# Four graph layers on one core: node tables beside the sort and in groups, with the near rows scattered behind all key rows

## The chip, the cores and the metric

One core of a Trainium2 chip runs the whole program. The metric is the device time of one execution in microseconds; the median over several executions is given.

## What is computed

Four graph layers run over N = 6250 nodes of 128 features and E = 206250 edges (src, dst, sorted by dst). The one whose start is changed is layer 0, whose softmax is over the edges of one source:

```python
x_i = x[dst]; x_j = x[src]
key = (x_i @ Wk + bk).reshape(-1, H, DH)
msg = (x_j @ Wm + bm).reshape(-1, H, DH)
query = (x_j @ Wq + bq).reshape(-1, H, DH) / jnp.sqrt(jnp.float32(DH))
scores = jnp.sum(query * key, axis=2)
smax = jax.ops.segment_max(scores, src, num_segments=N)
e = jnp.exp(scores - smax[src])
ssum = jax.ops.segment_sum(e, src, num_segments=N)
alpha = e / ssum[src] * cnt[src][:, None]
out = jax.ops.segment_sum((msg * alpha[:, :, None]).reshape(-1, D), dst, num_segments=N)
```

Layers 1 to 3 are an attention, a GAT and a weighted sum over the same edges, all summed by dst.

## The kernel before

Edges lie in SBUF as 128 partitions of T = 1612, once ordered by source (o = 0) and once by destination (o = 1). A pass (`pass_pool`, `pass_dve`, `pass_act`, `pass_sp`) walks along all partitions at once, in 62 turns of two halves of K = 13 edges. The row of the far end of each edge (k, q and m, and so on) is gathered by POOL, one indirect DMA per edge column, so 1612 in a pass (L1256). The row of the near end is the same along a segment: it stands once in a DRAM array of mostly zeros (`start_rows_by_src`, `start_rows_by_dst`), at the place of the segment's first edge, is read in order by SP (`near_load`) and is spread along the segment by a scan on DVE (`hold_rows`, L1312). Pass B runs by source and makes maximum and sum of each source; PA (same layer), P1, P2 and P3 run by destination.

Before pass B stands a preparation:

- `loads_sp`, `keys_dve`, `sort_dve`: keys (src, dst) are sorted by a bitonic network on 128 x 2048. DVE does the minima and maxima. For the steps across partitions PE turns the keys and ACT copies the half that DVE can't read from PSUM (`sort_act`, `sort_pe`, L709 and L723). There are 7 such stages (lp), each with two exchanges. The input is already sorted by dst, so a second sort (`unsorted`) is skipped.
- Beside it ACT, PE and SP make the q, k and m tables of layer 0 in 13 groups of 4 x 128 nodes (`proj0_sort_act`, `proj0_sp`). The order on ACT and PE is written out: `BEFORE_GROUP = {9: 1, 11: 2}` puts the exchanges of stage 1 ahead of group 9 and those of stage 2 ahead of group 11; the rest come behind group 12. SP writes zeros into the start-row array in between: 104 rows of 256 KB ahead of the groups (`zeros_sp`, L403), 5 behind each group, the rest behind the last.
- Behind the sort, `order_sp`, `order_dve`, `node_parts_dve`, `masks_dve` and `node_ends_dve` make the tables for each order: the restart masks of the scans, and for each of 6271 nodes where its segment begins (`spos`) and ends (`endix`). For this a node's partition is found by comparing the first key of each partition with all nodes (`cmp_n`, L1027 and L1029); that partition's key row (1612 int16) is gathered from DRAM by POOL, one gather for each 128 nodes (L1072), and ACT counts with a sign activation and accumulator how many keys lie below the node (`count_act`, L1077). By source the 52 gathers run in pairs of two buffers, with a staging copy of the index on POOL. By destination there is one gather and one count in each turn of pass B (L1262).
- `spread_sp` and `spread_pool` load q rows (before pass B) and k rows (behind it) back from DRAM and POOL scatters them, 49 x 128, to the beginnings of the segments (L1115).

Line 8 of `nodes_pool`, the wait that ties a pair of gathers to the counts two steps back, and in `pass_pool` the extra gather of pass B:

```python
g_.wait_ge(S(f"nt_counted{b}"), g * 2 + 2)
...
if q is PB and b:
    g_.wait_ge(S("nt_counted"), i + NB)
    g_.sem_inc(S("pool_go"), 1)
    g_.indirect_dma_start(row1, None, keyrow_t[1], bass.IndirectOffsetOnAxis(ap=row_i[:, 0:1], axis=0))
```

## Time and profile before

| | us |
|---|---|
| median of 3 executions | 11731.74 (11731.05 to 11731.93) |
| the profiled execution | 11731.4, its span 11729.7 |
| POOL busy, 8674 instructions | 8195.7 (70%) |
| DVE busy | 7246.8 (62%) |
| ACT busy | 5377.5 (46%) |
| PE busy | 1023.3 (9%) |
| first gather of pass B | at 772.29 |
| last key-row gather of pass B | at 2861.35 |
| first gather of pass A | at 3027.4 |

Time runs from the start of the span. "Busy" leaves out the time between two instructions of an engine, and for POOL each gather has 0.3 us of that. A timeline row has start, duration, engine, line, operation, and in brackets the idle time ahead of it and what ended it. The last part of the chain of waits (34% of the span) is POOL on L1256.

### The profile page before, as it was taken

The numbers are of one execution on the slowest core, as the hardware profiler recorded it, in microseconds if no ns is written. First come the engines' busy times: TensorE is split into PE (matmuls) and PEld (weight loads), VectorE is DVE, ScalarE is ACT, GpSimd is POOL, SyncE is SP. The second block draws the span as 40 slices with busy tenths as digits, with TensorE's granted clock in tenths as the row PEclk, the third lists the DMA queues.
The fourth block names the chain that finished last, engine by engine and source line by source line (L and its number), as shares of the span: only waits on it lengthen the run. The fifth ranks groups of instructions, "written<-read, shape, count | busy, mean of one in ns | idle before, by whom it ended". The sixth has DMA issues, their size and how long they took to land.

```text
span 11729.7 us, 40039 instructions
## 1 busy us (share of the span) xinstructions
PE 1023.3 (9%) x4194; PEld 843.3 (7%) x4194; DVE 7246.8 (62%) x7044; ACT 5377.5 (46%) x6052; POOL 8195.7 (70%) x8674
## 2 busy tenths in 40 slices
PE   4102222222000000040000000200000000000001
PEld 3002222222000000020000000200000000000001
DVE  9625555554588888848999999444444443333333
ACT  3134444443466666636666666233333333333332
POOL 0067777776777777747777776677777767777776
PEclk8555555555555555565555555555555555555555
DMA  7646666665466666636666666233333333333333
GB/s 260 221 148 209 204 211 207 206 211 173 145 213 213 214 214 214 213 103 211 223 221 222 222 222 208 71 112 113 112 111 112 112 95 105 105 105 105 105 105 105
DMA packets 791402, 1959.33 MB, mean 167 GB/s; under 512 B 213947, under 2 KB 419603, under 8 KB 790738
## 3 DMA queue, kind: packets, MB, share of 16 engines
q1 hardware_dynamic: 458010, 1136.08, 27.1%
q0 software_dynamic: 333184, 821.25, 25.2%
q14 instruction: 173, 1.42, 0.0%
q8 instruction: 35, 0.57, 0.0%
HBM read 1217.94 MB, written 738.73 MB: 167 GB/s over the span
## 4 chain that ended last, share of the span: by engine, by line
POOL 35%; DVE 19%; issue 15%; DMA 4%; PE 1%; ACT 1%; DVEq 0%; POOLq 0%; SPq 0%; ACTq 0%
POOL region L1256 34%; DVE work L1411 4%; DVE psB L1312 4%; DMA region<-x,ix_s 2%; DVE psR L1348 2%; DVE work L1344 2%; DVE psR L1404 2%; DVE psR L1396 2%; POOL work L1685 1%; PE psB L808 1%; DVE m_ext L1379 0%; POOL start_rows_by_dst L1115 0%; DVE psR L1357 0%; DMA region<-h,ix_s 0%; DVE psR L1382 0%
## 5 line engine op out<-in xcount | busy, mean ns | idle before, releaser
L1411 DVE TENSOR_TENSOR_SCAN work<-work,psR 128x1792 f32<-128x1792 f32 (+2 forms) x496 | 1971.2, 3974 | 92.5 <-DVE ix_s L1331 56.5
L1256 POOL DMA_INDIRECT region<-kv,ix_s x1612 | 1524.8, 946 | 497.6 <-issue 494.9
L1256 POOL DMA_INDIRECT region<-x,ix_s x1612 | 1521.0, 944 | 502.8 <-issue 458.4
L1256 POOL DMA_INDIRECT region<-qm,ix_s x1612 | 1524.0, 945 | 492.8 <-issue 489.8
L1256 POOL DMA_INDIRECT region<-k,ix_s x1612 | 1521.5, 944 | 491.3 <-issue 488.3
L1256 POOL DMA_INDIRECT region<-h,ix_s x1612 | 1521.0, 944 | 491.3 <-issue 488.8
L1312 DVE TENSOR_TENSOR_SCAN psB<-psB,work 128x1792 f32<-128x1792 f32 (+1 forms) x496 | 1485.0, 2994 | 549.8 <-ACT psB L1442 495.2
L1429 ACT COPY work<-region 128x1664 f32<-128x1664 f32 (+1 forms) x496 | 1164.2, 2347 | 1394.9 <-DMA region<-start_rows_by_dst 730.2
L1507 ACT COPY work<-work 128x1664 f32<-128x1664 f32 (+3 forms) x620 | 1573.4, 2538 | 0.0
L1506 ACT COPY psR<-work 128x128 f32<-128x128 f32 (+2 forms) x496 | 190.2, 384 | 2733.6 <-DVEq L1412 2733.6
L1344 DVE TENSOR_TENSOR work<-region,psB 128x1664 f32<-128x1664 f32 x372 | 702.0, 1887 | 770.6 <-DMA work<-keyrow,row_i 427.9
L1396 DVE TENSOR_TENSOR psR<-region,psB 128x1664 f32<-128x1664 f32 x124 | 235.1, 1896 | 1246.4 <-DMA region<-x,ix_s 1246.4
L1442 ACT ACTIVATE psB<-restart 128x1792 f32<-128x1792 bf16 (+1 forms) x496 | 647.4, 1305 | 15.6
L1404 DVE TENSOR_TENSOR psR<-region,psR 128x1664 f32<-128x1664 f32 x248 | 466.9, 1883 | 214.8 <-ACT work L1483 214.8
L1362 DVE TENSOR_TENSOR s_max<-region,psB 128x52 f32<-128x52 f32 x124 | 30.4, 245 | 740.9 <-DMA region<-h,ix_s 740.9
L1348 DVE TENSOR_REDUCE psR<-work 128x52 f32<-128x1664 f32 (+1 forms) x248 | 469.9, 1895 | 8.6
L1483 ACT ACTIVATE work<-dd 128x56 f32<-128x56 f32 (+2 forms) x372 | 463.0, 1245 | 0.0
L1068 POOL COPY half_i<-nt_i 128x2 int32 x26 | 17.9, 690 | 588.1 <-POOLq L1061 508.3
L1446 ACT ACTIVATE work<-restart 128x1792 f32<-128x1792 bf16 x248 | 417.7, 1684 | 0.0
L1647 PE MATMUL psR<-cst,contT 128*128 128x128 f32 x4 | 1.6, 502 | 4272.9 <-DVEq L1608 4272.9
L1650 PE MATMUL psR<-work,ones 128*128 128x512 f32 x8 | 7.9, 1120 | 4094.9 <-DVEq L1600 4094.9
L1154 PE MATMUL psR<-we,work 128*128 128x16 f32 x1612 | 355.2, 375 | 0.0
(306 smaller groups left out, 5345.9 us busy)
## 6 DMA issues: line engine op xcount, KB each, us to landing
region<-start_rows_by_dst SPq DMA_DIRECT2D x248, 832.0 KB, 6.6
state_p<-work SPq DMA_DIRECT2D x124, 936.0 KB, 4.8
state_p<-work SPq DMA_DIRECT2D x124, 884.0 KB, 3.9
region<-start_rows_by_src SPq DMA_DIRECT2D x124, 832.0 KB, 9.9
start_rows_by_dst<-zero_t SPq DMA_DIRECT2D x62, 1664.0 KB, 7.6
state_pA<-work SPq DMA_DIRECT2D x124, 832.0 KB, 4.9
state_p<-work SPq DMA_DIRECT2D x124, 832.0 KB, 3.5
start_rows_by_src<-zero_t SPq DMA_DIRECT2D x1, 59904.0 KB, 163.6
```

The costliest lines, as they stand in the source:

```text
L1256: g_.indirect_dma_start(rows_s[b][:, k, 0:wd_s], None, q.tabs, bass.IndirectOffsetOnAxis(ap=ix_s[b][:, k:k + 1], axis=0))\
L1312: nc.vector.tensor_tensor_scan(near_ps[:, 0:m], near_ps[:, 0:m], zt[:, 0:m], 0.0, ALU.mult, ALU.add).then_inc(q.s("held"), 1)
L1344: nc.vector.tensor_tensor(prod, rs[:, :, 0:D], hv[:, :, 1:K + 1].rearrange("p f t -> p t f"), ALU.mult).then_inc(q.s("dotted"), 1)
L1348: c.did(nc.vector.tensor_reduce(s.rearrange("p h t -> p t h"), prod.rearrange("p t (h d) -> p t h d", h=H), AX.X, ALU.add))
L1396: c.did(nc.vector.tensor_tensor(bvv[:, :, 1:K + 1].rearrange("p f t -> p t f"), rs[:, :, 0:D], w.unsqueeze(2).to_broadcast([P, K, D]), ALU ...
L1404: c.did(nc.vector.tensor_tensor(bvh[:, :, 0:dh, 1:K + 1].rearrange("p h j t -> p t h j"), rs[:, :, off:off + D].rearrange("p t (h j) -> p ...
L1411: c.do(nc.vector.tensor_tensor_scan(st[:, 0:F * (K + 1)], decay_at(q, b)[:, 0:F * (K + 1)], summed[:, 0:F * (K + 1)], 0.0, ALU.mult, ALU.add))
L1429: nc.scalar.copy(f_by_t(zt, q.HF)[:, :, 1:K + 1].rearrange("p f t -> p t f"), rows_d[b][:, :, :].rearrange("p t w -> p (t w)")[:, 0:K * q. ...
L1442: nc.scalar.activation(f_by_t(near_ps, q.HF), restart[q.o][:, bass.ds(n, 1), :].to_broadcast([P, q.HF, K + 1]), ACT.Exp).then_inc(q.s("mad ...
L1446: return nc.scalar.activation(f_by_t(decay_at(q, b), q.F), restart[q.o][:, bass.ds(n, 1), :].to_broadcast([P, q.F, K + 1]), ACT.Exp)
L1483: nc.scalar.activation(f_by_t(decay_at(q, b), F).rearrange("p (h j) t -> p h j t", h=H), heads(dd, q).unsqueeze(2).to_broadcast([P, H, dh ...
L1507: ins = nc.scalar.copy(pr[:, :, 0:F], stv[:, :, 1:K + 1].rearrange("p f t -> p t f"))
```

## The change

The load of the edge lists (`edges_in`) moves ahead of the sort, and is cut at partition 112. The tables by destination are made beside the sort: ACT converts the keys and finds the partitions with 49 small sign activations (`dst_act`), SP stores the key row behind the first zeros (`dst_keyrow_sp`), POOL gathers the 49 rows in four buffers (`dst_pool`), and ACT counts four in each projection group from group 1 on (`dst_count_act`). Q and k rows stay in SBUF (`near_qk`), so nothing is loaded back for the scatters; for this pass B gets buffers of its own (`spare`), and the m rows alternate in `tab`. SP writes four tables per group in place of three.

By source DVE compares in parts of 4, 8, 16, 16 and 5 columns (`PARTS`), POOL gathers in five buffers without a staging copy (`src_pool`), and positions are made group by group (`src_dve`), with the masks, counts and the bias addition put between the groups. `ROWS_LEAD = NG` sets how far the scatters stand behind the gathers: all 49 gathers first, then the 49 scatters. In pass B the key-row gather and its count are gone. Behind pass B `spread_dst_pool` scatters the k rows from SBUF.

```diff
+        PB.zt, PB.prod = spare(0, D * (K + 1)), spare(1792, K * D).rearrange("p (t f) -> p t f", f=D)
+        PB.bv, PB.abig, PB.st = [spare(8448 + i * few, few) for i in range(3)]
+        PB.psrow = psrow_src
...
+        PB.steps, PB.needs = 9, [("spread_out", 16 * NN)]
...
                 sp.dma_start(q.ps[EP:EP + 1, :], ctz[:, 0:q.W]).then_inc(S("dummy_rows"), 16)
+            edges_in(sp, (("dst", seg_i), ("src", oth_i[1])), S("edges_in"))
...
                 zeros_sp(sp, 0, ZERO_FIRST)
+                dst_keyrow_sp(sp, 0)
                 proj0_sp(sp)
                 zeros_sp(sp, ZERO_FIRST + NG * ZERO_BETWEEN, ZERO_ROWS)
...
                 if g < NG - 1:
                     normed0(act, g + 1)
+                if g:
+                    for j in range((g - 1) * BPG, g * BPG if g < NG - 1 else NN):
+                        dst_count_act(act, 0, j)
+                else:
+                    act.wait_ge(S("keys_out"), 16)
                 act.wait_ge(S("mm0"), g + 1)
...
-                nc.scalar.copy(tab0[g % 2].rearrange("p j (k d) -> p k j d", k=3), psB[:, 0:3, :].rearrange("p k (j d) -> p k j d", j=BPG)).then_inc(S("tab0"), 1)
...
+                nc.scalar.copy(near_qk[:, :, g * BPG:g * BPG + n, :], psB[:, 0:2, 0:n * D].rearrange("p k (j d) -> p k j d", d=D))
+                nc.scalar.copy(tab_m[g % 2][:, 0:n, :], psB[:, 2, 0:n * D].rearrange("p (j d) -> p j d", d=D)).then_inc(S("tab0"), 1)
...
                 sp.wait_ge(S("tab0"), g + 1)
-                sp.dma_start(rows_of(k0_t, g), t[:, 0:nb(g), 0:D]).then_inc(out0, 16)
-                sp.dma_start(rows_of(q0_t, g), t[:, 0:nb(g), D:2 * D]).then_inc(out0, 16)
-                sp.dma_start(rows_of(qm0_t, g)[:, :, 0:2 * D], t[:, 0:nb(g), D:3 * D]).then_inc(out0, 16)
+                sp.dma_start(rows_of(qm0_t, g)[:, :, D:2 * D], tab_m[g % 2][:, 0:nb(g), :]).then_inc(out0, 16)
+                sp.dma_start(rows_of(qm0_t, g)[:, :, 0:D], q_rows).then_inc(out0, 16)
+                sp.dma_start(rows_of(k0_t, g), k_rows).then_inc(out0, 16)
+                sp.dma_start(rows_of(q0_t, g), q_rows).then_inc(out0, 16)
                 zeros_sp(sp, ZERO_FIRST + g * ZERO_BETWEEN, ZERO_FIRST + (g + 1) * ZERO_BETWEEN)
...
-            sp.wait_ge(*table("segments", o))
-            sp.dma_start(keyrow_t[o], seg16).then_inc(S("keyrow_out"), 16)
...
         def edges_in(sp, what, sem):
 
             full, rest = E // T, E % T
             for name, dst in what:
-                sp.dma_start(dst[0:full, 0:T], A[name][0:full * T].rearrange("(p t) -> p t", t=T)).then_inc(sem, 16)
+                for a, z in ((0, full // 16 * 16), (full // 16 * 16, full)):
+                    sp.dma_start(dst[a:z, 0:T], A[name][a * T:z * T].rearrange("(p t) -> p t", t=T)).then_inc(sem, 16)
                 sp.dma_start(dst[full:full + 1, 0:rest], A[name][full * T:E].rearrange("(p t) -> p t", p=1)).then_inc(sem, 16)
...
+        def dst_act(act, again):
+
...
+                act.wait_ge(S("edges_in"), 96)
+                act.wait_ge(S("dummies"), DUMMIES + 1)
+            did(nc.scalar.copy(seg16[1].bitcast(I16), seg_i))
+            did(nc.scalar.copy(segf[1], seg_i))
+            do(nc.scalar.copy(head_i[1][:, :], seg_i[:, 0:1]))
+            if not again:
+                act.wait_ge(S("consts"), CONSTS)
+            did(nc.scalar.mul(diag2[:, 0, :], ident[:, :], segf[1][:, 0:1]))
+            do(nc.scalar.mul(diag2[:, 1, :], ident[:, :], segf[1][:, T - 1:T]))
+            act.wait_ge(S("dst_rows"), again + 1)
+            do(nc.scalar.copy(end_rows[1][:, :], psB[:, 0, 0:2 * P]))
+            for j in range(NN):
+                if j >= BPG:
+                    act.wait_ge(S("dst_steps"), steps[0] - BPG + 1)
+                did(nc.scalar.activation(hst[:, j % BPG, :], end_rows[1][:, 0:P], ACT.Sign, scale=-1.0, bias=nt_b[:, j:j + 1], accum_out=nt_q[1][:, j:j + 1]))
+            act.wait_ge(S("dst_steps"), steps[0])
+            do(nc.scalar.activation(nt_q[1][:, 0:NN], nt_q[1][:, 0:NN], ACT.Relu, scale=0.5, bias=half_p[:, 0:1]))
+            did(nc.scalar.copy(nt_i[1][:, 0:NN], nt_q[1][:, 0:NN]))
+            assert steps[0] == base + DST_STEPS, steps
...
+        def dst_keyrow_sp(sp, again):
+            sp.wait_ge(S("dst_steps"), again * DST_STEPS + 1)
+            sp.dma_start(keyrow_t[1], seg16[1].bitcast(I16)).then_inc(S("keyrow_out"), 16)
+
+        def dst_pool(g_, again):
+
+            g_.wait_ge(S("keys_made"), 1)
+            g_.wait_ge(S("keyrow_out"), 16 * (again + 1))
+            g_.wait_ge(S("dst_steps"), (again + 1) * DST_STEPS)
+            for j in range(NN):
+                if j >= 4:
+                    g_.wait_ge(S("nt_counted"), again * NN + j - 3)
+                g_.indirect_dma_start(dst_rows[j % 4], None, keyrow_t[1], bass.IndirectOffsetOnAxis(ap=nt_i[1][:, j:j + 1], axis=0))\
+                  .then_inc(S(f"row_in{j % 4}"), 16)
+
+        def dst_count_act(act, again, j):
+            r = j % 4
+            act.wait_ge(S(f"row_in{r}"), 16 * (again * DST_IN[r] + j // 4 + 1))
+            if again * NN + j:
+                act.wait_ge(S("nt_counted"), again * NN + j)
+            nc.scalar.activation(unread_signs[1], dst_rows[r], ACT.Sign, scale=-1.0, bias=nt_b[:, j:j + 1],
+                                 accum_out=nt_c[1][:, j + 1:j + 2]).then_inc(S("nt_counted"), 1)
...
+        PARTS = [0, 4, 12, 28, 44, NN]
...
+        def src_sp(sp):
+            sp.dma_start(raw_src, sorted_dram[0, 0:EP].bitcast(I32).rearrange("(p t) -> p t", t=T)).then_inc(S("raw_in"), 16)
+            sp.wait_ge(S("tables_made"), 2)
+            sp.dma_start(keyrow_t[0], seg16[0].bitcast(I16)).then_inc(S("keyrow_out"), 16)
...
+        def src_act(act):
+            for j in range(NN):
+                r = j % 5
+                act.wait_ge(S(f"src_row{r}"), 16 * (j // 5 + 1))
+                act.wait_ge(S("nt_counted"), 2 * NN + j)
+                nc.scalar.activation(unread_signs[0], src_rows[r], ACT.Sign, scale=-1.0, bias=nt_b[:, j:j + 1],
+                                     accum_out=nt_c[0][:, j + 1:j + 2]).then_inc(S("nt_counted"), 1)
+
+        def src_pool(g_):
+
+            proj0_wait(g_)
+            g_.wait_ge(S("keyrow_out"), 48)
+            chunk = 0
+            for g in range(NG + ROWS_LEAD):
+                if g < NG:
+                    for j in range(g * BPG, g * BPG + nb(g)):
+                        if j == PARTS[chunk]:
+                            chunk += 1
+                            g_.wait_ge(S("tables_made"), 2 + chunk)
+                        if j >= 5:
+                            g_.wait_ge(S("nt_counted"), 2 * NN + j - 4)
+                        g_.indirect_dma_start(src_rows[j % 5], None, keyrow_t[0], bass.IndirectOffsetOnAxis(ap=nt_i[0][:, j:j + 1], axis=0))\
+                          .then_inc(S(f"src_row{j % 5}"), 16)
+                if g == ROWS_LEAD:
+                    g_.wait_ge(S("zeroed"), 16 * NZEROS)
+                if g >= ROWS_LEAD:
+                    k = g - ROWS_LEAD
+                    g_.wait_ge(S("nodes_ready"), k + 1)
+                    for j in range(k * BPG, k * BPG + nb(k)):
+                        g_.indirect_dma_start(qxb_t, bass.IndirectOffsetOnAxis(ap=spos[0][:, j:j + 1], axis=0), near_qk[:, 0, j, :], None).then_inc(S("spread_out"), 16)
+
+        def spread_dst_pool(g_):
+            g_.wait_ge(S("zeroed_a"), 16 * (IT // 2))
+            for j in range(NN):
+                g_.indirect_dma_start(qxa_t, bass.IndirectOffsetOnAxis(ap=spos[1][:, j:j + 1], axis=0), near_qk[:, 1, j, :], None).then_inc(S("spread_out"), 16)
...
+            v.wait_ge(S("raw_in"), 32)
+            for h in range(2):
+                c = h * (T - 1)
+                q.did(nc.vector.tensor_scalar(ends_i[:, h:h + 1], raw_src[:, c:c + 1], 13, 0x1FFF, ALU.logical_shift_right, ALU.bitwise_and))
+            q.wait()
+            q.do(nc.vector.tensor_copy(ends_f[:, :], ends_i[:, :]))
...
+            q.do(nc.vector.tensor_scalar(seg_i, raw_src, 13, 0x1FFF, ALU.logical_shift_right, ALU.bitwise_and))
+            q.do(nc.vector.tensor_copy(seg16[0].bitcast(I16), seg_i))
             v.sem_inc(S("tables_made"), 1)
-            v.wait_ge(S("ends_rows"), o + 1)
-            q.do(nc.vector.tensor_copy(firstrow[:, :], psC[:, 0:P]))
...
+            def parts(i):
+                a, z = PARTS[i], PARTS[i + 1]
+                n = z - a
+                to = cmp_n[:, 0:n * P].rearrange("p (j r) -> p j r", r=P)
+                q.do(nc.vector.tensor_tensor(to, end_rows[0][:, 0:P].unsqueeze(1).to_broadcast([P, n, P]),
+                                             nid[:, a:z].unsqueeze(2).to_broadcast([P, n, P]), ALU.is_le))
+                q.do(nc.vector.tensor_reduce(nt_q[0][:, a:z], to, AX.X, ALU.add))
+                q.do(nc.vector.tensor_scalar(nt_q[0][:, a:z], nt_q[0][:, a:z], -1.0, 0.0, ALU.add, ALU.max))
+                q.do(nc.vector.tensor_copy(nt_i[0][:, a:z], nt_q[0][:, a:z]))
+                v.sem_inc(S("tables_made"), 1)
...
+            beside = {0: rest_of_keys, 1: lambda: masks_dve(v, q, 0), 2: counts, DST_AT: lambda: ends_up_to_dve(v, q, 1, 0, NN),
+                      DST_AT + 1: dst_begins, 5: lambda: masks_dve(v, q, 1), 6: lambda: bias_dve(v, b2_0, q)}
...
+                ends_up_to_dve(v, q, 0, a, z)
+                if g in beside:
+                    beside[g]()
+                v.wait_ge(S("nt_prev"), g + 1 + (g > DST_AT))
+                begins_dve(v, q, 0, a, z, psD[:, a:z])
+
...
-                    if q is PB and b:
-
-                        g_.wait_ge(S("nt_counted"), i + NB)
-                        g_.sem_inc(S("pool_go"), 1)
-                        g_.indirect_dma_start(row1, None, keyrow_t[1], bass.IndirectOffsetOnAxis(ap=row_i[:, 0:1], axis=0)).then_inc(q.own(f"rows{b}"), 16)
...
+            if q in (PB, PA):
+                v.wait_ge(S("spread_out"), (16, 32)[q.o] * NN)
...
-            order_sp(sp, 0)
-            order_sp(sp, 1)
-            spread_sp(sp, 0, q0_t)
+                again_sp(sp)
...
+            src_sp(sp)
             pass_sp(sp, PB)
-            spread_sp(sp, 1, k0_t)
...
-            nodes_pool(g_)
-            spread_pool(g_, 0, qxb_t)
+            dst_pool(g_, 0)
...
+            src_pool(g_)
             pass_pool(g_, PB)
-            spread_pool(g_, 1, qxa_t)
+            spread_dst_pool(g_)
...
-            order_dve(v, 0)
-            node_parts_dve(v, 0)
-            masks_dve(v, 0)
-            order_dve(v, 1)
-            node_parts_dve(v, 1)
-            masks_dve(v, 1)
-            bias_dve(v, b2_0)
-            node_ends_dve(v, 0)
...
+            src_dve(v)
             pass_dve(v, PB)
-            node_ends_dve(v, 1)
...
+            dst_act(act, 0)
             proj0_sort_act(act)
...
-            nodes_act(act)
...
+            src_act(act)
```

POOL from the constants to the end of pass B's loop, before (rows of the loop body; `half_i` is the staged index):

```order
L1068 COPY half_i<-nt_i 128x2
L1069 REGISTER_ALU
L1072 DMA work<-keyrow,half_i 128x1612 x2
L1068 ISA
L1068 COPY half_i<-nt_i 128x2
L1072 DMA work<-keyrow,half_i 128x1612 x2
L1064 REGISTER_ALU
L1064 COMPARE_AND_BRANCH
L1115 DMA start_rows_by_src<-region,spos 212992x128 x49
L1248 DMA head<-q,head_i 128x128
```

and now, in the same place (`nt_i` is the table of partitions):

```order
L1112 DMA work<-keyrow,nt_i 128x1612 x2
L1112 DMA region<-keyrow,nt_i 128x1612 x2
L1112 DMA tab<-keyrow,nt_i 128x1612
L1112 DMA work<-keyrow,nt_i 128x1612 x2
L1112 DMA region<-keyrow,nt_i 128x1612 x2
L1120 DMA start_rows_by_src<-work,spos 212992x128 x49
L1345 DMA head<-q,head_i 128x128
L1346 UNCONDITIONAL_BRANCH
L1346 ISA
L1353 DMA region<-k,ix_s 128x128 x26
L1346 REGISTER_ALU
L1346 COMPARE_AND_BRANCH
```

The loop with its copies is gone, the index comes straight out of the table, and the body of pass B has 26 gathers and no key row.

ACT in one group of the projection beside the sort, before:

```order
L870 COPY hT<-psB 128x512 [waits tr0]
L855 ACTIVATE hst<-xsb,ln_a 128x128 x4
L876 COPY work<-psB 128x3x4x128 [waits mm0]
L870 COPY hT<-psB 128x512 [waits tr0]
L855 ACTIVATE hst<-xsb,ln_a 128x128 x4
```

and now:

```order
L896 COPY hT<-psB 128x512 [waits tr0]
L881 ACTIVATE hst<-xsb,ln_a 128x128 x4
L1041 ACTIVATE region,nt_c<-region,nt_b 128x1612 [waits nt_counted,row_in0]
L1041 ACTIVATE region,nt_c<-region,nt_b 128x1612 [waits nt_counted,row_in1]
L1041 ACTIVATE region,nt_c<-region,nt_b 128x1612 [waits nt_counted,row_in2]
L1041 ACTIVATE region,nt_c<-region,nt_b 128x1612 [waits nt_counted,row_in3]
L908 COPY work<-psB 128x2x512 [waits j0_out0,mm0]
L909 COPY tab<-psB 128x512
L896 COPY hT<-psB 128x512 [waits tr0]
```

Four counts, each waiting for a row, stand between the normalization of the next group and the copy out of PSUM.

## Rows read from the trace of the kernel before

**Rows 1.** ACT in the projection beside the sort, timeline (start us, us, engine line op)
```profile
106.02 1.65 ACT L855 ACTIVATE hst<-xsb,ln_a 128x128 f32<-128x128 f32 x4 [36.38 <-DVEq L832]
...
119.31 1.44 ACT L876 COPY tab<-psB 128x1536 f32<-128x1536 f32 x1 [8.25 <-PE psB L896]
...
121.12 1.65 ACT L855 ACTIVATE hst<-xsb,ln_a 128x128 f32<-128x128 f32 x4
129.83 1.44 ACT L876 COPY work<-psB 128x1536 f32<-128x1536 f32 x1 [7.05 <-PE psB L896]
...
199.06 0.65 ACT L709 COPY work<-psR 128x512 f32<-128x512 f32 x1
```

**Rows 2.** DVE at the sort's first exchange through PE, timeline
```profile
199.75 0.60 DVE L624 SCALAR_TENSOR_TENSOR region<-work,psR 128x256 f32<-128x256 f32 x1 [0.88 <-ACT work L709]
```

**Rows 3.** from the sort's end to the first key-row gather, timeline
```profile
492.06 1.00 DVE L965 TENSOR_SCALAR region<-region 128x1612 int32<-128x1612 int32 x1 [9.80 <-DMA region<-keys_sorted]
...
496.06 0.32 SPq L949 DMA_DIRECT2D keyrow<-region  x1
...
515.23 1.14 POOL L1072 DMA_INDIRECT work<-keyrow,half_i  x1 [0.92 <-POOL half_i L1068]
```

**Rows 4.** source view of the key-row gathers (ns min/median/max, first and last start us)
```profile
L1072 POOL DMA_INDIRECT work<-keyrow,half_i x52: 942/967/3287, 515.2 to 694.7; - x52
...
DMA to landing us min/median/max: 3.8/4.7/9.7
```

**Rows 5.** the first counts on ACT, timeline
```profile
522.15 1.64 ACT L1077 ACTIVATE work<-work,nt_b 128x1612 f32<-128x1612 int16 x1 [65.15 <-DMA work<-keyrow,half_i]
...
523.91 1.64 ACT L1077 ACTIVATE work<-work,nt_b 128x1612 f32<-128x1612 int16 x1
```

**Rows 6.** scatters of near rows (source view), then the pass's first gather (timeline)
```profile
L1115 POOL DMA_INDIRECT start_rows_by_src<-region,spos x49: 965/969/1003, 706.7 to 767.9; - x49
...
772.29 0.96 POOL L1256 DMA_INDIRECT region<-k,ix_s  x1 [0.30 <-issue]
```

**Rows 7.** POOL in pass B and behind it: source view, then timeline
```profile
L1256 POOL DMA_INDIRECT region<-k,ix_s x1612: 940/944/989, 772.3 to 2860.1; - x180
...
2861.35 0.95 POOL L1262 DMA_INDIRECT work<-keyrow,row_i  x1 [0.30 <-issue]
...
2890.09 1.00 POOL L1115 DMA_INDIRECT start_rows_by_dst<-region,spos  x1 [27.79 <-DMA region<-k]
```

**Rows 8.** one half of pass B on DVE, product to held-row scan, timeline
```profile
2846.32 1.89 DVE L1344 TENSOR_TENSOR work<-region,psB 128x1664 f32<-128x1664 f32 x1 [0.59 <-DMA region<-k,ix_s]
...
2854.20 3.90 DVE L1312 TENSOR_TENSOR_SCAN psB<-psB,work 128x1792 f32<-128x1792 f32 x1 [2.47 <-ACT psB L1442]
```

**Rows 9.** DMA issues, first 800 us (KB each, us to landing)
```profile
keyrow<-region SPq DMA_DIRECT2D x2, 403.0 KB, 2.9
```

**Rows 10.** stores of k rows beside the sort, source view
```profile
L908 SPq DMA_DIRECT2D k<-tab x7: 333/360/827, 120.8 to 266.3; - x7
...
DMA to landing us min/median/max: 1.5/2.3/9.6
```

**Rows 11.** windows table: busy us (x) by engine, PEclk, DMA share, GB/s
```profile
60.00:70.00 10.00, 0.00 (x0) 0.00 (x0) 9.86 (x12) 9.61 (x44) 0.00 (x0) 1.00 1.03 387
160.00:170.00 10.00, 8.34 (x36) 5.87 (x37) 9.86 (x9) 4.62 (x9) 0.00 (x0) 0.83 0.68 236
```

**Rows 12.** POOL's gathers under DVE operations, timeline
```profile
520.09 1.03 POOL L1072 DMA_INDIRECT work<-keyrow,half_i  x1 [0.79 <-POOL half_i L1068]
...
520.44 3.52 DVE L1012 TENSOR_TENSOR_SCAN ew<-region,ones 128x1612 f32<-128x1612 f32 x1
...
646.47 1.83 DVE L1000 TENSOR_TENSOR region<-region 128x1611 f32<-128x1611 f32 x1
...
647.21 1.94 POOL L1072 DMA_INDIRECT work<-keyrow,half_i  x1 [0.79 <-POOL half_i L1068]
```

**Rows 13.** DVE behind the load of both edge lists, timeline
```profile
624.14 1.00 DVE L982 CAST region<-region 128x1612 int16<-128x1612 int32 x1 [98.19 <-DMA oth_i<-in_src_dram]
```

More of the change, by code:

```diff
@@ new lines, in src_dve @@
+        def src_dve(v):
+            q = line(v)
+            v.wait_ge(S("nt_counted"), 2 * NN)
+            v.wait_ge(S("dst_steps"), 2 * DST_STEPS)
+            proj0_wait(v)
+            v.wait_ge(S("raw_in"), 32)
[4 more added lines that the diff above has]
+            q.do(nc.vector.tensor_copy(ends_f[:, :], ends_i[:, :]))
+            for h in range(2):
+                q.did(nc.vector.tensor_scalar(diag2[:, h, :], ident[:, :], ends_f[:, h:h + 1], None, ALU.mult))
+            q.wait()
```

367 lines of the change are left out of this document (169 added, 198 removed).

## The prediction

> **What bounds the kernel now.** I read the profile from coarse to fine: first the windows table of the first 5,400 us, to see which engine is full in which stretch, then the timeline at each border, then the source view of the lines that the change touches, for durations and for the time from issue to landing. From the first gather of pass A at 3,027 us on, almost nothing is changed (only the load of `ew` is cut into three transfers), so four stretches matter.
> (1) The sort, to 482.26 us. DVE works back to back. Beside it ACT runs the 13 groups of the first projection: from one copy out of PSUM to the end of the next normalization 3.46 us of its own work, then 7.05 us of waiting for PE [rows 1]. DVE comes to its first exchange through PE at 198.9, ACT ends group 8 at 199.1: neither waits for the other [rows 1, 2]. That is the place where extra work on ACT begins to count.
> (2) 482.26 to 772.29, the tables by source and their scatter. The first key-row gather goes out at 515.23 [rows 3], the 52 take until 694.7, 3.5 us each [rows 4], though ACT needs only 1.76 us from one count to the next [rows 5]: with pairs of rows in two buffers it waits for landings. Then 49 scatters, 1.275 us each, and 772.29 is the first gather of the pass [rows 6].
> (3) Pass B, 772.29 to 2862.6. 1612 table gathers and 62 key-row gathers leave POOL without a gap: 2087.8 us over 1672 intervals is 1.249 us each [rows 7]. POOL's issue is the bound.
> (4) 2862.6 (2861.35 + 0.94 + 0.30) to 2890.09: POOL stands still until DVE has made the positions by destination and SP has loaded the k rows back [rows 7].
>
> **The sum, part by part.**
> *Pass B without its key rows.* 62 x 1.249 = **77.4 us** less, if POOL stays the bound. The other loop of one half runs from the product on DVE to the end of the next scan of held rows: 2846.32 to 2858.10, 11.8 us, where POOL's 13 gathers take 16.2 [rows 8]. So all of it counts; the count on ACT, which leaves too, had been hidden. Bounds: 77.4, and 0 if another loop takes over.
> *The gap behind pass B.* The k rows stay in SBUF and the positions are made long before. The scatters follow the last gather: 2890.09 - 2862.6 = **27.5 us** less. The 49 scatters cost what they did. Carry and end gathers follow behind them as before. What hides the last results of DVE and ACT is these 62 us of scatters; the wait for the last chunk of zeros is met earlier. Bounds 20 and 27.5.
> *Sort's end to pass B.* Keys out and in again take 9.8 us as before, the new key row leaves SP at about 496.5 [rows 3], and lands 2.9 later [rows 9]. Only 4 columns of the comparison stand ahead of the first gather, no longer 52, so it goes out at 499.5. Its row lands 3.8 us after issue at the soonest [rows 4]: ACT begins at 503.5. From there 49 counts at 1.76. Five rows in flight give POOL 8.8 us to replace one, against 4.7 of median landing, so ACT should be the bound; but DVE holds POOL back at times (below: a scan of 3.5 us, a bias addition of 7.1), and I add 5 us. The last gather is issued when 44 are counted, the scatters go out at 503.5 + 77.4 + 5 + 1.3 = 587.2 and end at 649.7; the positions of the last group, ready near 599, are needed only at 648. From the last scatter's end to the first gather 3.1 us as before: 652.8 for 772.29, **119.5 us** less. Bounds: 124.5 with no such hold, and 38 if rows come no faster than the 3.5 us of now. I take the value near the ACT bound because the two things that made 3.5, pairs and the staging copy, are both gone.
> *The sort is held up.* This is the price. ACT now counts 4 rows by destination in each group from group 1 on. The first index table costs nothing: some 25 us of ACT work (49 small signs at about 0.4, two copies of 1.5) fall into a wait of 36.4 us that ends at 106.02 [rows 1]. But the key row by destination is stored on SP's queue behind 26,624 KB of zeros (104 x 128 x 2 KB). A 256 KB store given to that queue at 120.8 landed 9.6 us later, at 130.4, where the usual one takes 2.3 [rows 10]; so the queue is served in order and drains at 130. Ahead of the zeros there are now 1.6 MB of edges, 4.2 us at 387 GB/s [rows 11]. POOL's first gather: 134.5. First row landed at about 140, four counted at 147.8, group 1 out at 149.3 where it was 131.3. Then seven groups of 3.46 + 7.04 + 0.1 = 10.6 us: group 8 ends at 223.5, the first exchange waits 24.5 us. Behind it groups 9 and 10 fit into ACT's idle time there, and 11 and 12 into their waits for PE. For traffic I add 3.5: a group's stores and zeros already keep the DMA engines 0.68 busy [rows 11], and four rows of 0.41 MB in 10.6 us are 156 GB/s, 0.42 more, so rows and stores will crowd each other. **28 us** more. Bounds: 19, if PE's pace of 9.8 us a group holds, and 55, if rows come at 3.5 us (14 us a group, and 4 to 7 us at the later exchanges).
> *Sum.* 11731.4 - 77.4 - 27.5 - 119.5 + 28 = **11535 us**. The profiled execution (11731.4, span 11729.7) stands 0.3 below the median of the runs, so I correct nothing.
>
> **A port that decides two of the terms.** A gather that POOL issued while DVE compared two SBUF operands (646.47 to 648.30) took 1.94 us in place of 0.97, and ended 0.85 behind DVE [rows 12]. The other way round, a 3.52 us scan that DVE began in the middle of such an issue was not longer per column (2.18 ns) than the scan of 3.90 over 1792 columns [rows 8, 12]. So I expect the 49 issues in the sort, where every DVE operation reads SBUF twice, to take 1.4 to 2.1 us, under the 2.65 that a group leaves for each, and DVE to lose next to nothing. The Trainium skill (SBUF — State Buffer, "Who interferes with whom") says that a DVE instruction with two SBUF inputs contends with a GpSimd instruction that reads SBUF, and that whoever issues first has the shared ports for the whole instruction. On POOL's side the trace agrees; that DVE is held for all of POOL's instruction it does not show. By that rule to the letter the sum would be 11554 instead of 11535.
>
> **Rivals.**
> - *DVE pays for POOL's issues too* (0.12). 32 issues before the first exchange hold DVE 0.97 each: it arrives at 230, later than ACT, 31 us; 17 more cost 16.5. The hold is 47.5, the time 11554. Against it stands the scan just named, a single one.
> - *POOL starves beside the sort* (0.07). Between two sort operations there is hardly a gap; if POOL is let in only when DVE stands, the rows of groups 1 to 8 are counted while DVE waits (8 x 10.6 + 5 = 90), those of two groups at each of the next two exchanges (35 in all): 125 us of hold, 11632. Against: behind DVE's comparison POOL ended 0.85 later although DVE went on at once.
> - *The sort is hardly held* (0.08), under 10 us, because zeros and the key row overtake: 11513. Against it, the 9.6.
> - *Edges load slowly* (0.04). Now both lists, 127 partitions at a time, kept DVE waiting 98.2 us [rows 13]. If the cut into 112 and 15 partitions doesn't help, the store of the keys and the zeros start 94 us later: 11629. The Trainium skill (DMA: Bandwidth & Descriptors, on how many engines a DMA uses) has 127 partitions on one engine, 112 on 16 and 15 on 15, which would leave this rival out; the 1.6 MB in 98.2 us, 16 GB/s, agrees for the 127.
> - *Rows by source come no faster than now* (0.06): 81 us of the 119.5 stay, 11616.
> - *The change doesn't do in pass B what it says* (0.05): the loop of one half stretches, POOL waits for free buffers, and the 77.4 stay: 11612.
> - *Slower than before* (0.01): all 49 rows by destination must be counted before ACT frees the third exchange, which came at 268.9. If landings in the crowded stretch stretch to t us a row, the hold is 134.5 + 49 t - 268.9; it eats all gains (224.4) from t = 7.3 us on. At 8 us it is 258 us, and the time 11765. Even the longest landing seen, 9.7 us [rows 4], gives (1.3 + 9.7 + 1.8) / 4 = 3.2 with four in flight.
>
> **How the numbers follow.** The forecast, 11535, has 0.57; its own range is 11515 to 11560 (holds of 19 to 55 against 0 to 10 us of delays by the port behind the sort). The range that should hold 8 in 10 takes in the rivals at 11513, 11554, 11612 and 11616: 11505 to 11617, and leaves out starving, slow edges and slower, 0.12, and some tail. 0.2% of the time is 23 us, about what a measurement can tell from no change; every case but the last is far more than that below: faster 0.98, same 0.01, slower 0.01.
>
> **What would show it.** DVE idle some 25 us before the sort's first exchange and next to nothing at the later ones; sort's end near 510; key-row gathers by source over about 85 us, ACT nearly full there; first pass-B gather near 681; 1612 gathers at 1.249 us with nothing between, ended near 2693; scatters by destination at once behind; from there the chain of waits as before, 196 us earlier. I am wrong if DVE's own operations in the sort grow longer, if it waits at several exchanges, or if POOL idles in pass B.

## The result, and the profile after

The changed kernel takes **11539.1 us** (median of 4 executions, 11536.31 to 11542.82) where the one before takes 11731.83: a ratio of 0.9835 (95% interval 0.9818 to 0.9852). The forecast was 11535, with a range of 11505 to 11617. The profiled execution took 11536.31, its span 11534.5. Executions of one kernel lie up to 12 us apart and a ratio's interval is some 15 to 20 us to either side, so differences of 10 us between the kernels below are read from the stages of their traces; the medians only have to agree.

| stage, by the traces | before | after | change | forecast |
|---|---|---|---|---|
| start to the sort's end | 482.3 | 516.7 | +34.4 | +28 |
| sort's end to the first gather of pass B | 290.0 | 174.2 | -115.8 | -119.5 |
| pass B, first gather to the end of the last | 2090.3 | 2012.5 | -77.8 | -77.4 |
| gap ahead of the scatters by destination | 27.5 | 0.1 | -27.4 | -27.5 |
| these scatters to the first gather of pass A | 137.3 | 138.9 | +1.6 | 0 |
| pass A and its end, to the first gather of P1 | 2259.3 | 2252.4 | -6.9 | 0 |
| the rest | 6443.0 | 6439.7 | -3.3 | 0 |
| sum | 11729.7 | 11534.5 | -195.2 | -196.4 |

The sum came out within 1.2 us of the forecast because +6.4 and +3.7 were balanced by stages that were costed at nothing (+1.6, -6.9 and -3.3). That it came so close is luck; what held is the stages, each to within 7 us.

The price is paid where it was looked for, ahead of the first exchange. DVE after, in the timeline (beside [rows 2], where it had waited 0.88):

```profile
234.03 0.61 DVE L649 SCALAR_TENSOR_TENSOR region<-work,psR 128x256 f32<-128x256 f32 x1 [35.59 <-ACT work L734]
...
269.09 0.42 DVE L649 SCALAR_TENSOR_TENSOR region<-work,psR 128x256 f32<-128x256 f32 x1 [1.51 <-ACT work L734]
...
304.77 0.42 DVE L649 SCALAR_TENSOR_TENSOR region<-work,psR 128x256 f32<-128x256 f32 x1 [1.48 <-ACT work L734]
```

35.59 once, and 1.5 at the exchanges behind it, as in the kernel before. How the 35.6 came about is told by SP's queue, POOL and ACT after, timeline:

```profile
56.90 2.12 SPq L422 DMA_DIRECT2D start_rows_by_src<-zero_t  x1
70.27 59.57 SPq L1023 DMA_DIRECT2D keyrow<-region  x1
129.88 1.24 SPq L941 DMA_DIRECT2D qm<-tab  x1
```
```profile
140.00 1.62 POOL L1033 DMA_INDIRECT region<-keyrow,nt_i  x1 [134.47 <-DMA keyrow<-region]
```
```profile
105.54 1.65 ACT L881 ACTIVATE hst<-xsb,ln_a 128x128 f32<-128x128 f32 x4 [11.24 <-DVEq L858]
...
148.62 1.64 ACT L1041 ACTIVATE region<-region,nt_b 128x1612 bf16<-128x1612 int16 x1 [26.40 <-DMA region<-keyrow,nt_i]
...
155.72 0.99 ACT L908 COPY work<-psB 128x1024 f32<-128x1024 f32 x1
...
232.01 0.99 ACT L908 COPY work<-psB 128x1024 f32<-128x1024 f32 x1
```

The index table was free, as costed: 11.2 us of ACT's old wait of 36.4 are left. The store of the key row kept SP's queue 59.6 us behind the zeros. ACT had the first row 26.4 us after it was ready for it, and then took (232.01 - 155.72) / 7 = 10.9 us a group.

That DVE itself pays nothing for POOL's 49 issues in the sort is seen in the groups of its instructions over the sort, before and after:

```profile
L620 DVE TENSOR_TENSOR region<-region 128x1024 f32<-128x1024 f32 (+1 forms) x159 | 180.8, 1137 | 5.0
```
```profile
L645 DVE TENSOR_TENSOR region<-region 128x1024 f32<-128x1024 f32 (+1 forms) x159 | 180.8, 1137 | 5.0
```

The same 159 operations, the same 180.8 us. Behind the sort, the source views of the gathers, the scatters and pass B (beside [rows 4, 6, 7]):

```profile
L1112 POOL DMA_INDIRECT work<-keyrow,nt_i x20: 942/946/2437, 534.5 to 621.1; - x20
L1112 POOL DMA_INDIRECT region<-keyrow,nt_i x20: 944/947/7416, 537.1 to 624.7; - x20
...
```
```profile
L1120 POOL DMA_INDIRECT start_rows_by_src<-work,spos x49: 965/969/1005, 626.0 to 687.1; - x49
```
```profile
L1353 POOL DMA_INDIRECT region<-k,ix_s x1612: 940/944/967, 690.9 to 2702.2; - x180
```
```profile
L1125 POOL DMA_INDIRECT start_rows_by_dst<-work,spos x49: 965/969/1395, 2703.5 to 2765.1; - x49
```

49 rows in 90.2 us where 52 took 179.5; the pass at 1.248 us a gather without a gap; the scatters by destination right behind it. One gather took 7.4 us. It stood beside DVE's bias addition:

```profile
593.91 7.42 POOL L1112 DMA_INDIRECT region<-keyrow,nt_i  x1 [0.30 <-issue]
```
```profile
593.41 7.09 DVE L1805 TENSOR_TENSOR xsb<-xsb,b 128x6656 f32<-128x6656 f32 x1
```

It ended 0.83 us behind the addition, as the 0.85 of [rows 12] would have it. ACT had other rows to count for 6.5 us of this, then stood until the late one had landed:

```profile
604.30 1.64 ACT L1096 ACTIVATE region<-region,nt_b 128x1612 bf16<-128x1612 int16 x1 [3.90 <-DMA region<-keyrow,nt_i]
```

### The profile page after: what moved, and what is told of

Same layout as the page of the kernel before. It is cut to its first block, busy times and chain, and to the rows that moved or that the text cites. A ratio compares the mean times of both kernels' runs of the same rounds, so it can differ in the third digit from the quotient of the medians.

```text
span 11534.5 us, 40086 instructions
## 1 busy us (share of the span) xinstructions
PE 1036.4 (9%) x4242; PEld 851.2 (7%) x4242; DVE 7235.1 (63%) x7083; ACT 5376.6 (47%) x6139; POOL 8188.7 (71%) x8632
## 3 DMA queue, kind: packets, MB, share of 16 engines
q1 hardware_dynamic: 461412, 1129.66, 27.4%
## 4 chain that ended last, share of the span: by engine, by line
POOL 50%; DVE 21%; issue 20%; DMA 4%; ACT 2%; PE 1%; another core or an unknown queue 1%; DVEq 0%; POOLq 0%; SPq 0%; ACTq 0%
POOL region L1353 47%; DVE work L1498 5%; DVE psB L1403 4%; DMA region<-x,ix_s 2%; DVE psR L1491 2%; DVE work L1431 2%; DVE psR L1435 2%; DVE psR L1483 2%; POOL work L1768 1%; DVE region L645 1%; DVE region L646 1%; PE psB L834 1%; DVE m_ext L1466 0%; POOL start_rows_by_dst L1125 0%
## 5 line engine op out<-in xcount | busy, mean ns | idle before, releaser
L1590 ACT COPY work<-work 128x1664 f32<-128x1664 f32 (+2 forms) x496 | 1539.2, 3103 | 0.0
L1254 PEld LDWEIGHTS psR<-we,work 128*128 128x128 f32 x1612 | 348.5, 331 | 30.4 <-issue 30.4
```

What stands on the lines that cost most here:

```text
L1254: ins = nc.tensor.matmul(sum_ps[:, PAY_AT + u * 16:PAY_AT + (u + 1) * 16], attrT[:, u, :], we2[:, :], start=False, stop=u == KE // 2 - 1)
L1590: ins = nc.scalar.copy(pr[:, :, 0:F], stv[:, :, 1:K + 1].rearrange("p f t -> p t f"))
```

## The experiments

Theory: the hold of the sort is ACT's, made of a late first row (SP's queue, served in order, with the zeros ahead) and of counts ahead of the exchange; behind the sort ACT sets the pace of the rows and POOL that of all else. Rivals stand with each run. "Less" and "more" are against the changed kernel's 11539.1.

**The key row ahead of most zeros.**

```diff
-                zeros_sp(sp, 0, ZERO_FIRST)
-                dst_keyrow_sp(sp, 0)
+                zeros_sp(sp, 0, 16)
+                dst_keyrow_sp(sp, 0)
+                zeros_sp(sp, 16, ZERO_FIRST)
```

> The key row by destination is stored behind 16 rows of zeros instead of 104. If its place in SP's queue is what made the first count late (148.6), the row is in DRAM by about 85, POOL's first gather follows the index table at about 94, and the counts of group 1 begin without a wait at 122.2: 26 us earlier than in the changed kernel. DVE then waits 9 to 10 us at the first exchange instead of 35.6, and the time is 26 us less, about 11513. Rival: in the crowd of the zeros each row by destination lands so late that ACT waits in every group; then DVE still waits over 20 us at the first exchange and the gain is under 15 us.

Measured: 11530.1 (11527.2 to 11534.6), 9 less. The row landed 8.5 us after its issue at 70.2, POOL gathered from 94.8, ACT counted from 122.29 without a wait. Yet DVE still waited 25.2 us. The rival had the amount but not the reason; SP and ACT of this run:

```profile
120.41 19.43 SPq L942 DMA_DIRECT2D qm<-tab  x1
```
```profile
129.46 1.01 ACT L909 COPY work<-psB 128x1024 f32<-128x1024 f32 x1
...
154.71 1.01 ACT L909 COPY work<-psB 128x1024 f32<-128x1024 f32 x1 [13.23 <-DMA q<-work]
```

Group 2 waits for the stores of group 0 (its table buffer), and these are now what stands behind the zeros. In the changed kernel that second wait lay under the first.

**The key row on ACT's own queue.** ACT gives the transfer itself, behind its conversion; SP keeps its 104 rows of zeros ahead of the groups.

```diff
+            nc.scalar.dma_start(keyrow_t[1], seg16[1].bitcast(I16)).then_inc(S("keyrow_out"), 16)
...
-            sp.dma_start(keyrow_t[1], seg16[1].bitcast(I16)).then_inc(S("keyrow_out"), 16)
```

> The key row by destination is given to ACT's queue by ACT itself, behind the conversion; SP's queue keeps 104 rows of zeros ahead of the groups. If only the order within SP's queue made the row late, a second queue gets its share beside the zeros: the row lands within some 10 us of its issue (before 85), POOL gathers from 94 on, and the rest is as in the run with the early key row, group 2 waiting for the stores of group 0: about 11530. Rival: the DMA engines work off what was given first, whatever the queue; then the row still lands near 139 and the time stays at 11539.

Measured: 11528.2 (11524.3 to 11531.4), first gather at 95.1, group 2 waiting 13.36 us for its stores. The DMA issues of this run up to 200 us (KB, us from issue to landing):

```profile
keyrow<-region ACTq DMA_DIRECT2D x1, 403.0 KB, 6.8
```

On SP's queue it had been 68.9. The DMA engines moved 385 GB/s from 60 to 100 us here, as in the changed kernel (384). So it is the order within one queue, not the load of the DMA engines, that made the row late.

**Fewer zeros ahead of everything.**

```diff
-        ZERO_FIRST, ZERO_BETWEEN = 104, 5
+        ZERO_FIRST, ZERO_BETWEEN = 40, 5
```

> The changed kernel with 40 rows of zeros ahead of the key row and the groups instead of 104; the other 64 go out behind the last group. If SP's queue, served in order, is what delays first the key row (landing at 139) and, once that is early, the stores of group 0 that group 2 waits for (13.2 us in the run with the early key row), then 10.5 MB at 387 GB/s are through by about 85, POOL gathers from 94 on, ACT counts group 1 from 122.3 without a wait and group 2 does not wait either. With 10.6 us a group ACT reaches the first exchange at about 205: DVE waits 7 to 8 us, the time is 27 us less, about 11512. Rival: group 2's wait was the work of rows and stores crowding the DMA engines, not of the queue; then it stays and the time is that of the early key row alone, about 11530.

Measured: 11513.1 (11512.3 to 11517.2), 26 less. No group waits for stores, and DVE:

```profile
207.80 0.60 DVE L649 SCALAR_TENSOR_TENSOR region<-work,psR 128x256 f32<-128x256 f32 x1 [9.04 <-ACT work L734]
```

One number gives back three quarters of what the sort had lost. SP's queue is blocked for a shorter time too, 14.7 us in place of 59.6:

```profile
70.62 14.73 SPq L1023 DMA_DIRECT2D keyrow<-region  x1
```

The 9.04 that stay are the counts only in part. With the counts moved as well, three of the runs below (with 40 or 48 rows of zeros ahead) still wait 2.75, 5.10 and 0.65 us, for PE's pace; the difference, 4 to 8 us, is an estimate of what the counts cost.

**Counts behind the first exchange.**

```diff
-                if g:
-                    for j in range((g - 1) * BPG, g * BPG if g < NG - 1 else NN):
-                        dst_count_act(act, 0, j)
+                for j in range(max(0, g - 9) * 4, max(0, g - 8) * 4):
+                    dst_count_act(act, 0, j)
...
                 sort_act(act, 0, lp)
+                for j in range(16 + (lp - 3) * 8, min(24 + (lp - 3) * 8, NN)):
+                    dst_count_act(act, 0, j)
```

> No count stands in groups 0 to 8; four stand in each of groups 9 to 12 and the other 33 behind the exchanges of stages 3 to 7, eight at a time (14.6 us of ACT where it had waited 28). If the counts on ACT ahead of the first exchange are the whole price of the sort, DVE reaches it at 198.4 and waits about 1 us, no later exchange gets a longer wait, the sort ends at 482 to 483, and the time is 34 us less, about 11505. Rival 1: POOL's issues or the extra traffic lengthen DVE's own operations or the exchanges; then less than 20 us come back. Rival 2: the counts behind the later exchanges hold them up; the wait reappears there, some us at each.

Measured: 11515.9 (11512.3 to 11524.2), 23 less. Both rivals fall: the later exchanges kept their 1.5 us with eight counts ahead of each, and DVE's operations in the sort kept their mean (1138 ns for 1137). But at the first DVE still waited 10.44 us, and ACT shows the same second wait, with no count near it:

```profile
143.82 1.01 ACT L907 COPY work<-psB 128x1024 f32<-128x1024 f32 x1 [10.99 <-DMA q<-work]
```

**Edge lists uncut.** `edges_in` gives one transfer over 127 partitions for each list, so the load of `ew` behind pass A is uncut too.

```diff
-                for a, z in ((0, full // 16 * 16), (full // 16 * 16, full)):
+                for a, z in ((0, full),):
...
```

> Each edge list is loaded by one transfer over 127 partitions instead of one over 112 and one over 15. If that form moves 16 GB/s, as behind the sort in the kernel before, the lists are in at about 142 (43.5 + 98). ACT, which needs them for the index table at about 66, waits some 76 us, all projection groups come that much later, and DVE waits about 110 us at the first exchange: the time is 70 to 80 us more, 11609 to 11619. If the transfers ahead hold up the whole queue, zeros and the copy of the keys too, it is 94 us more. Rival: the cut does nothing by itself and the 98 us before were contention behind the sort; then the time does not change.

Measured: 11603.8 (11598.8 to 11606.4), 65 more:

```profile
58.15 30.91 SPq L971 DMA_DIRECT2D oth_i<-in_src_dram  x1
```
```profile
108.70 1.53 ACT L997 CAST region<-region 128x1612 int16<-128x1612 int32 x1 [39.76 <-DMA oth_i<-in_src_dram]
```
```profile
288.87 0.60 DVE L649 SCALAR_TENSOR_TENSOR region<-work,psR 128x256 f32<-128x256 f32 x1 [90.37 <-ACT work L734]
```

The lists were in 65 us after their issue, not 98, so ACT waited 39.8 us where I had reckoned 76; but SP's queue stood too, the zeros began at 111.8 instead of 56.9, and the first row was gathered at 194.8 in place of 140.0. These 54.8 us are what DVE's wait grew by. That the cut matters is shown; the 70 to 80 us expected were near the 65, but by a wait of ACT for the lists, when it was the queue behind them that decided.

**A gather put back into pass B.**

```diff
+                    if q is PB and b:
+                        g_.indirect_dma_start(back[:, :].bitcast(I16), None, keyrow_t[1], bass.IndirectOffsetOnAxis(ap=nt_i[1][:, 0:1], axis=0)).then_inc(q.own(f"rows{b}"), 16)
...
-                v.wait_ge(q.own(f"rows{b}"), i * (16 * K) + 16 * K)
+                rows = K + (q is PB and b)
+                v.wait_ge(q.own(f"rows{b}"), i * (16 * rows) + 16 * rows)
```

> One gather of a key row (not counted by anyone) is put back at the end of each of the 62 turns of pass B. If POOL's issue is the bound, each costs a full 1.249 us: 77.4 us more, about 11616, POOL without gaps in the pass. Rival: the loop of DVE, ACT and the landings had become the bound once the key rows were gone; then a part of the 62 disappears in gaps and the time grows by less than 60 us.

Measured: 11617.9 (11612.6 to 11621.0), 78.8 more. The pass, from 692.8 to 2782.9, is 77.6 us longer. The group of the added gathers, busy time, mean and idle time ahead of them:

```profile
L1357 POOL DMA_INDIRECT back<-keyrow,nt_i x62 | 58.6, 945 | 18.9 <-issue 18.9
```

(58.6 + 18.9) / 62 = 1.25 us each, and nothing of it hidden.

**Three rows in flight.** The five buffers of `src_rows` become three, with the waits on them.

```diff
...
-                        if j >= 5:
-                            g_.wait_ge(S("nt_counted"), 2 * NN + j - 4)
+                        if j >= 3:
+                            g_.wait_ge(S("nt_counted"), 2 * NN + j - 2)
...
```

> Key rows by source in three buffers instead of five. A buffer is taken again when its row has landed (4.7 us behind the issue) and been counted (1.82): three in flight give one row in (4.7 + 1.82 + 0.1) / 3 = 2.2 us instead of the 1.84 measured with five, where ACT is the bound: 49 x 0.36 = 18 us more, about 11557. Rival: POOL or DVE sets the pace of the rows, not the landings; then three buffers do as well as five and the time stays at 11539.

Measured: 11562.0 (11557.9 to 11565.6), 23 more. First to last gather 108.9 us, 2.27 a row. ACT now idles ahead of nearly every count. Its idle time by what ended it, and how often, in the source view of the counts:

```profile
  DMA work<-keyrow,nt_i: 66.1, 29
  DMA region<-keyrow,nt_i: 7.1, 15
```

Less the 47 us ahead of the first count, which the changed kernel has too, that is 26 us. With three buffers the pace is near landing plus count over rows in flight, (4.7 + 1.82 + 0.1) / 3 = 2.2; with five ACT is the bound.

**Scatters two groups behind the gathers.**

```diff
-        ROWS_LEAD = NG
+        ROWS_LEAD = 2
```

> ROWS_LEAD = 2: the scatters of q rows stand two groups behind the gathers of key rows instead of behind all of them. Gathers alone are paced by ACT (1.82 us a row), so POOL has 0.6 us a row to spare, 28 us over all 49, which scatters can fill: 49 x (1.25 + 1.27) = 123.5 us of issues instead of 152.6 from the first gather to the last scatter. But POOL is then the bound, and what DVE's two-input operations hold it (some 18 us beyond 0.95 in the 49 gathers of the changed kernel) counts in full: 141 us, 11 to 12 us less, time about 11527. If those holds do not add up, it is 29 us less, 11510. Rival: scatters wait for positions at each group (counts, PE and six DVE operations behind the last row of a group) and the gathers behind them are held up too; then nothing is gained, 11539 or more.

Measured: 11528.3 (11526.9 to 11534.8), 11 less. From the first gather to pass B 145.0 us instead of 156.4. No scatter waited for its positions:

```profile
L1120 POOL DMA_INDIRECT start_rows_by_src<-work,spos x49: 965/972/2496, 554.0 to 676.3; - x49
```
```profile
609.26 6.80 POOL L1112 DMA_INDIRECT tab<-keyrow,nt_i  x1 [0.31 <-issue]
```

POOL issues nearly back to back, and what holds an issue now counts in full, above all the 6.80 beside the bias addition. Five rows in flight had hidden a part of that hold: in the changed kernel the issue took 7.42 and ACT stood for 3.90.

**Three edits together** (late counts, 40 and 5 rows of zeros, `ROWS_LEAD = 2`).

> Three edits together: counts by destination behind group 8 as in the run with late counts, 40 rows of zeros ahead of the groups, scatters two groups behind the gathers. The late counts alone gave 11516, with 10.4 us of waiting left at the first exchange, of which a group's wait for its stores behind the zeros was the cause: with the shorter queue 1 to 3 us remain, 8 less. The scatters between the gathers give what they give alone. If the three add up: 11516 - 8 - 12 = 11496; if the scatters gain nothing: 11508.

Measured: 11511.7 (11507.4 to 11515.9), where 11496 had been expected. The first exchange is nearly free (2.75), yet:

```profile
483.53 10.72 SPq L761 DMA_DIRECT2D keys_sorted<-region  x1
```
```profile
511.07 0.15 DVE L1156 TENSOR_SCALAR ends_i<-region 128x1 int32<-128x1 int32 x1 [27.57 <-DMA region<-keys_sorted]
```

The zeros that were moved out of the way in front now ended behind the sort, and the store of the sorted keys stood behind them: 27.57 us where it had been 10.78. In the windows table the DMA engines are still full from 480 to 500 us (engine columns as below, then granted clock, DMA share, GB/s):

```profile
480.00:500.00 20.00, 0.00 (x0) 0.00 (x0) 3.47 (x3) 0.00 (x0) 0.00 (x0) 0.50 1.04 388
```

It is the same queue, a third time.

**The zeros spread.** 48 rows ahead and 8 behind each group, the rest as in the run before.

> As the three edits together, but with 48 rows of zeros ahead of the groups and 8 behind each, so that the rest behind group 12 is 251 rows and not 298. In that run the store of the sorted keys sat behind the last zeros (DVE waited 27.6 us for the keys instead of 10.8). With 47 rows less there (12.3 MB, 31 us at 400 GB/s) the zeros end by about 470, before the sort, and the wait is 10.8 again: 16.8 less than 11511.7, about 11495. Rival: eight rows behind each group delay the stores and so ACT; then the wait at the first exchange grows beyond 2.8 us by as much.

Measured: 11496.0 (11492.3 to 11500.5). DVE waits 10.83 us for the keys, as expected, and 5.10 at the first exchange, 2.35 more than in the run before it. That is not the rival: no group waited for its stores, ACT waited for PE in each (5.2 to 7.1 us), and the next run, with the same zeros, waits 0.65.

**The bias addition in DVE's gap.**

```diff
+            bias_dve(v, b2_0, q)
             v.wait_ge(S("raw_in"), 32)
```

> As the run before it, with DVE's bias addition (7.1 us, two operands in SBUF) put into the 10.8 us in which DVE waits for the sorted keys, so that it is no longer beside POOL's issues. With scatters between the gathers POOL has no slack, and one gather took 6.80 us under that addition instead of 0.95: 5.9 us less, about 11489. Rival: POOL's long issue only covers time in which it would have waited for something else; then no gain, 11495.

Measured: 11491.7 (11491.3 to 11495.4), ratio to the kernel before 0.9795 (0.9782 to 0.9809). The addition:

```profile
487.74 7.09 DVE L1807 TENSOR_TENSOR xsb<-xsb,b 128x6656 f32<-128x6656 f32 x1 [5.72 <-issue]
```

It began only 5.72 us after DVE's last sort operation and ended at 494.83, 2.0 us later than the keys would have let DVE go on; the first gather comes 19.3 us behind the sort in place of 17.9. From there to pass B it is 4.7 us less (139.6). From the sort's end to pass B that makes 3.3 us gained (158.9 for 162.2), not 5.9. Of the 6.6 us between the two spans 2.7 lie ahead of the sort's end, where the first exchange came 4.2 us sooner by another pace of PE; the last 0.6 lie behind the start of pass B. The windows from 120 to 200 of the run before it and of this one (busy us and count of PE, weight load, DVE, ACT and POOL, granted clock, DMA share, GB/s):

```profile
120.00:200.00 80.00, 71.58 (x264) 50.29 (x264) 77.38 (x72) 27.57 (x56) 0.00 (x0) 0.69 0.88 294
```
```profile
120.00:200.00 80.00, 70.52 (x283) 50.60 (x284) 78.26 (x74) 28.85 (x58) 0.00 (x0) 0.74 0.95 320
```

The granted clock is a mean between its two levels (1.2 and 2.4 GHz): a group took 10.5 to 10.6 us where its mean was 0.66 to 0.68, and 8.6 to 8.9 where it was 0.77 to 0.83. The second run had more of the short ones, and PE got through 283 products in place of 264. The edit stands behind the sort, so this part is taken as chance, and the 4.3 us between the medians don't settle what the edit is worth. That the edits together beat the changed kernel is settled: its interval (0.9818 to 0.9852) lies wholly above this one.

## Why the prediction was right, point by point

*Pass B without key rows* (-77.4): -77.8, and 77.6 when a gather was put back. *The gap* (-27.5): -27.4; the scatters hid what was to be hidden.

*Sort's end to pass B* (-119.5): 3.7 us too much. The first gather came 17.8 us behind the sort (forecast 17.2), and the stretch behind the last gather was 0.7 us shorter. Between first and last gather 90.2 us passed, not 86.4: the term that was too small is the 1.76 us a count. The distance is 1.82, 2.6 us over the 44 counts ahead of the last gather. In the kernel before one wait let two counts go, here each waits for its own row and writes bf16 in place of f32; which of these makes the 0.06 was not separated. The allowance of 5 us for the port was near the size: ACT's counts took 6 us beyond 48 x 1.82, 3.9 of them for the row behind the bias addition.

*The sort is held up* (+28): +34.4. The mechanism stood, queue, first row, paced groups; three terms were small by a little. The edges ahead of the zeros cost 8.1 us (56.90; before, 48.79), not 4.2: the zeros wait for the copy of the keys, which now had the lists ahead of it and took 10.5 us where it had taken 4.2. The first row landed 8.6 us behind its issue, not 5.5. A group took 10.9, not 10.6. Together ACT came at 233.4, not 223.5 (the zeros drained another 1.6 us late, and four counts took 0.7 less). The 3.5 us for traffic took up a third of it, by luck: up to the first exchange ACT waited for no row but the first, and of the seven groups five took 10.5 to 10.6 us, while the two of 11.3 and 12.2 waited for PE (0.69 and 1.63). What the prediction did not see at all is the wait of group 2 for its stores; it cost nothing here, being under the first, and was worth 11 to 13 us as soon as that went.

*The port.* DVE's operations in the sort kept their mean, and the addition took 7.09 us beside a gather (above) and 7.09 alone in the last run, so the rival in which DVE pays (0.12) is refuted, as is starving (0.07). What did not come is the forecast that all 49 issues in the sort take 1.4 to 2.1 us. Of the 35 beside DVE's operations 19 were held (1.39 to 1.98 us, all but the first of them ended 0.81 to 0.83 behind the DVE operation in which they began), and 16 were not (0.94 to 1.02). One of each, after:

```profile
141.82 1.22 DVE L646 TENSOR_TENSOR region<-region 128x1024 f32<-128x1024 f32 x1
141.93 1.94 POOL L1033 DMA_INDIRECT region<-keyrow,nt_i  x1 [0.30 <-issue]
...
144.18 0.95 POOL L1033 DMA_INDIRECT region<-keyrow,nt_i  x1 [0.30 <-issue]
144.22 1.22 DVE L646 TENSOR_TENSOR region<-region 128x1024 f32<-128x1024 f32 x1
```

It cost nothing either way, since ACT and not POOL paced these rows. The Trainium skill (SBUF — State Buffer, "Who interferes with whom") has whoever issues first hold the shared ports for its whole instruction. Where DVE was first the trace agrees; where the gather was first, as at 144.18, DVE's operation was not longer. Only DVE operations that began within 0.02 us of a gather were longer, by 0.03 to 0.06 us: four in three traces, one of them in the changed kernel.

*Slow edges* (0.04) are real without the cut: 65 us. The Trainium skill (DMA: Bandwidth & Descriptors, "Why a DMA increments its semaphore by 16 and not by 1", on how many engines a DMA uses) puts 127 partitions on one engine and, by its rule, 112 on 16; the two runs agree in direction, and a rate for one engine can't be taken from them (1.6 MB took 65 us here and 98.2 in [rows 13]).

*The range.* The prediction's own range, 11515 to 11560, does not follow from its terms: holds of 19 to 55 us and delays of 0 to 10 give 11521 to 11567. The result lies in both.

*What was costed at nothing.* The prediction named the cut of the load of `ew` and gave it no price. It was some 5 us. This load starts while POOL carries the last state of pass A over. POOL before, then after, then with the list uncut:

```profile
5070.33 0.98 POOL L1641 DMA_INDIRECT state_pA<-prow,patch_i  x1 [4.85 <-DVEq L1633]
5075.80 0.97 POOL L1685 DMA_INDIRECT work<-state_pA,endix  x1 [4.48 <-DMA state_pA<-prow,patch_i]
```
```profile
4883.51 0.98 POOL L1724 DMA_INDIRECT state_pA<-prow,patch_i  x1 [2.87 <-DVEq L1716]
4886.03 0.97 POOL L1768 DMA_INDIRECT work<-state_pA,endix  x1 [1.53 <-DMA state_pA<-prow,patch_i]
```
```profile
4939.78 0.98 POOL L1724 DMA_INDIRECT state_pA<-prow,patch_i  x1 [4.75 <-DVEq L1716]
4945.25 0.97 POOL L1768 DMA_INDIRECT work<-state_pA,endix  x1 [4.48 <-DMA state_pA<-prow,patch_i]
```

POOL's two waits for the carry, which end with small transfers, are together 4.8 to 4.9 us longer beside the uncut load, in both kernels that have it. From the first gather of pass A to that of P1 these two take 2259.3 and 2258.0 us, the eleven others traced between 2250.5 and 2254.9. The further 2 us and the +1.6 behind pass B were not looked into; the -3.3 of the rest is less than the 6.7 us by which that stage varies among the traces.

## What to carry to other kernels

A store that somebody waits for must not be given to a queue behind bulk work, however idle the data are; and taking one such wait away shows the next on the same queue, so move the bulk work to where nothing urgent is given behind it, at its end too. Where one wait lies under another, taking away the upper one gives back only what the lower does not claim (9 us of 26, until both were gone). An engine with slack hides a part of what holds it, and filling the slack brings all of that into the sum.

## What had not been expected

A second queue was served beside the zeros at once (the row landed in 6.8 us, where SP's queue had taken 68.9), although the DMA engines moved 385 GB/s from 60 to 100 us of that run. An instruction that only gives a transfer occupied SP's queue for 59.6 us behind 104 rows of zeros, for 14.7 behind 40 and for 0.3 behind 16; what it waits for the traces don't say. And a load of 0.8 MB over 127 partitions made two waits for transfers of one index column each, on another queue, longer by 4.9 us together.
